# Set-up in order of need in a one-core transformer block kernel

## The reference

```python
out = jnp.einsum('bnd,ed->bne', patches, W) + b + pos
q, k, v = src @ Wq.T + bq, src @ Wk.T + bk, src @ Wv.T + bv
scores = jnp.einsum('bid,bjd->bij', q, k) / sqrt(64)
out = softmax(scores) @ v @ Wo.T + bo      # rows masked where q or k is 0 in column 0
h = layernorm(h + attention(h))
h = layernorm(h + ffn(h))    # top-1 of 8 experts, relu, capacity, weight by the gate
```

## Time and profile before

| | |
|---|---|
| median of 3 runs | 1059.79 us (1058.4 to 1060.67) |
| profiled execution | 1059.04 us, of which span 1057.1 us |
| instructions | 19754 |
| PE / DVE / ACT / POOL busy | 90% / 82% / 67% / 60% of the span |
| first set-up step of DVE | 9.67 us |
| first query-key product on PE | 14.25 us |
| first row maximum on DVE | 27.79 us |
| first product of scores on PE | 42.38 us |

### The profile page before, as it was taken

How to read it: one execution, slowest core, us unless ns; L and a number is a source line. 1 busy time by engine, 2 the same in 40 slices (tenths; PEclk the granted TensorE clock), 3 DMA queues, 4 the chain that set the end, 5 groups by cost and what they waited for, 6 DMA issues and landing times.

```text
span 1057.1 us, 19754 instructions
## 1 busy us (share of the span) xinstructions
PE 947.4 (90%) x6046; PEld 530.7 (50%) x6046; DVE 871.8 (82%) x1711; ACT 712.3 (67%) x1254; POOL 635.8 (60%) x624
## 2 busy tenths in 40 slices
PE   3799999999999999999999999999999999856740
PEld 2355545555555555555555555555555555433420
DVE  3667788789999999999999999999999999675561
ACT  2366655777777777777777777777777776636650
POOL 0004443346666666667776766666666777776775
PEclk9699999999999999999999999999999999958875
DMA  3332224333334333343334333433334332236200
GB/s 95 80 73 58 59 59 107 91 100 101 98 86 120 89 107 99 89 106 103 103 99 107 102 99 86 120 88 107 98 91 106 102 99 72 71 92 177 71 20 10
DMA packets 72504, 96.25 MB, mean 91 GB/s; under 512 B 15923, under 2 KB 52230, under 8 KB 72398
## 3 DMA queue, kind: packets, MB, share of 16 engines
q1 hardware_dynamic: 55566, 77.87, 29.0%
q0 software_dynamic: 16832, 17.11, 5.0%
HBM read 43.68 MB, written 18.11 MB: 58 GB/s over the span
## 4 chain that ended last, share of the span: by engine, by line
PE 48%; DVE 34%; issue 9%; ACT 7%; DMA 1%; POOL 1%; SPq 0%; POOLq 0%; ACTq 0%; DVEq 0%
PE p_u L603 12%; DVE mx L1031 9%; PE p_st L581 8%; PE p_misc L618 6%; PE p_misc L549 4%; PE p_misc L666 3%; PE p_sm L563 3%; PE p_misc L526 3%; ACT uu L809 3%; PE p_st L585 3%; DVE qk L1016 2%; DVE lo L1023 2%; ACT b_h L855 2%; PE p_sm L682 2%; PE p_misc L682 2%
## 5 line engine op out<-in xcount | busy, mean ns | idle before, releaser
L1411 POOL DMA_INDIRECT slots<-rows,idx x256 | 251.9, 984 | 186.2 <-issue 139.6
L1424 POOL DMA_INDIRECT out<-b_o,b_ix x270 | 303.8, 1125 | 98.0 <-issue 74.1
L1031 DVE TENSOR_REDUCE mx<-p_sm 128x1 f32<-128x1024 f32 x252 | 307.1, 1219 | 33.2 <-PE p_sm L565 30.1
L804 ACT ACTIVATE pT<-p_st 128x1024 f32<-128x1024 f32 x256 | 261.9, 1023 | 94.0 <-PE p_st L587 80.1
L603 PE MATMUL p_u<-pT,vv 128*64 128x512 f32 x1024 | 253.5, 605 | 0.0
L581 PE MATMUL p_st<-hi,hx 64*128 64x512 f32 x256 | 126.6, 495 | 8.6 <-ACT pT L804 4.4
L583 PE MATMUL p_st<-hx,hi 64*128 64x512 f32 x256 | 127.1, 496 | 0.0
L603 PEld LDWEIGHTS p_u<-pT,vv 128*64 128x64 f32 x1024 | 61.6, 136 | 104.7 <-issue 92.7
L581 PEld LDWEIGHTS p_st<-hi,hx 64*128 64x128 f32 x256 | 46.9, 183 | 131.3 <-issue 104.0
L563 PE MATMUL p_sm<-kh,hi 64*128 64x512 f32 x252 | 102.4, 406 | 6.1 <-DMA hx<-hi 3.5
L855 ACT ACTIVATE b_h<-p_misc,b_w 128x256 f32<-128x256 f32 x244 | 95.8, 475 | 13.5 <-PE p_misc L666 7.1
(11 more groups left out here) (191 smaller groups left out, 1869.7 us busy)
## 6 DMA issues: line engine op xcount, KB each, us to landing
b_w<-in_w SPq DMA_DIRECT2D x136, 193.5 KB
hx<-hi SPq DMA_DIRECT2D x64, 256.0 KB, 3.4
b_in<-slots SPq DMA_DIRECT2D x136, 66.0 KB
lx<-lo SPq DMA_DIRECT2D x32, 256.0 KB, 3.2
xt<-in_x SPq DMA_DIRECT2D x32, 196.0 KB
out<-b_o,b_ix POOLq DMA_INDIRECT x270, 2.3
kh<-kh SPq DMA_DIRECT2D x32, 128.0 KB, 2.3
lx<-lo SPq DMA_DIRECT2D x32, 128.0 KB, 3.2
```

Of the source, the lines that this page charges most:

```text
L804: act.activation(pT[k % 4][:, :], flat(p_st), ACT.Exp).then_inc(exp_done, 1)
L1031: dve.tensor_reduce(mx[:, p, at:at + 1], flat(max_place(n, j)), AX.X, ALU.max).then_inc(max_done, 1)
L1411: pool.indirect_dma_start(slots, bass.IndirectOffsetOnAxis(ap=idx[:, p, j:j + 1], axis=0), rows[:, p, j, :], None, bounds_check=SLOTS - 1, ...
L1424: pool.indirect_dma_start(out_rows, bass.IndirectOffsetOnAxis(ap=b_ix[:, o, j:j + 1], axis=0), b_o[:, o, j, :], None, bounds_check=T - 1, ...
```

## The change

Loads are issued in another order and with signals of their own: `c_deep` and `w_qk` (`deep_loaded`), the position table for tile 0 alone (`pos_loaded`), the patches of image 0, then `c_wide` and the positions of tiles 1 and 2 (`w_loaded`, now two transfers). The set-up makes `w_qkx` in its first round; the products behind `w_cg`, `w_lj`, `w_all` and `w_px` move behind the first query-key product. The constants that come from `c_wide` are made last. `key_steps(0)` moves in between. The first of image 0's two `hx` transfers has a semaphore of its own. `project(0, .., 1)` is cut into two halves at k = 2 and 3. Identity blocks of `w_lj` come from `c_deep`.

```diff
--- before.py
+++ after.py
@@ -264,10 +264,13 @@
             return back_place(c).rearrange("p (j u d) -> p u j d", j=CT, d=D)
 
 
+        deep_loaded = sem("deep_loaded")
+        pos_loaded = sem("pos_loaded")
         w_loaded = sem("w_loaded")
         x_loaded = [sem(f"x_loaded{i}") for i in range(3)]
         spread_kh = [sem(f"spread_kh{i}") for i in range(2)]
         spread_hi = [sem(f"spread_hi{i}") for i in range(3)]
+        spread_first = sem("spread_first")
         spread_lo = [sem(f"spread_lo{i}") for i in range(3)]
         free_stored = sem("free_stored")
         table_step = sem("table_step")
@@ -337,7 +340,7 @@
         last_rows_ready = sem("last_rows_ready")
         POOL_SET = 2
         GS = 13
-        NW = 4
+        NW = 2
 
         def of_parity(n, p, per):
 
@@ -388,10 +391,12 @@
         @block.sync
         def _(sp):
 
+            sp.dma_start(c_deep[:, :], deep).then_inc(deep_loaded, 16)
+            sp.dma_start(w_qk[:, :], wqk).then_inc(deep_loaded, 16)
+            sp.dma_start(xt[0:D, 0, :], posT).then_inc(pos_loaded, 16)
             sp.dma_start(xt[KA:KTOK, 0, :], x[0, :, :]).then_inc(x_loaded[0], 16)
-            for dst, src in ((c_deep[:, :], deep), (w_qk[:, :], wqk),
-                             (xt[0:D, :, :], posT.unsqueeze(1).broadcast_to([D, 3, S])), (c_wide[:, :], wide)):
-                sp.dma_start(dst, src).then_inc(w_loaded, 16)
+            sp.dma_start(c_wide[:, :], wide).then_inc(w_loaded, 16)
+            sp.dma_start(xt[0:D, 1:3, :], posT.unsqueeze(1).broadcast_to([D, 2, S])).then_inc(w_loaded, 16)
             for n in (1, 2):
                 sp.dma_start(xt[KA:KTOK, n, :], x[n, :, :]).then_inc(x_loaded[n], 16)
 
@@ -455,8 +460,9 @@
                 sp.wait_ge(hi_ready, n + 1)
                 if n >= 3:
                     sp.wait_ge(st_done, NT * (n - 2))
-                for dst, src in ((hx[t][D:P, :], hi[t][0:D, :]), (hx[t][0:D, :], hi[t][D:P, :])):
-                    sp.dma_start(dst.bitcast(F32), src.bitcast(F32)).then_inc(spread_hi[t], 16)
+                sp.dma_start(hx[t][D:P, :].bitcast(F32), hi[t][0:D, :].bitcast(F32))\
+                    .then_inc(spread_first if n == 0 else spread_hi[t], 16)
+                sp.dma_start(hx[t][0:D, :].bitcast(F32), hi[t][D:P, :].bitcast(F32)).then_inc(spread_hi[t], 16)
 
             def spread_low(n):
                 t = n % 3
@@ -495,27 +501,36 @@
         @block.tensor
         def _(pe):
 
-            pe.wait_ge(w_loaded, 16 * NW)
+            pe.wait_ge(deep_loaded, 32)
             pe.wait_ge(setup_v, 1)
-            pe.matmul(p_misc[0:D, 0, 0:D], w_v[:, :], w_oTp[:, :], start=True, stop=True)
-            pe.matmul(p_misc[0:D, 1, 0:E], c_centre[:, :], w_g[:, :], start=True, stop=True)
-            pe.matmul(p_sm[0:D, 0, 0:1], w_oTp[:, :], w_bv[:, :], start=True, stop=True)\
+            pe.matmul(p_u[0:KTOK, 0, 0:2 * D], w_e[:, :], w_qk[:, :], start=True, stop=True)\
                 .then_inc(setup_p, 1)
             pe.wait_ge(setup_v, 2)
-            pe.matmul(p_st[0:KA, 0, 0:CG], w_bl[:, :], w_cg[:, :], start=True, stop=True)
-            pe.matmul(p_st[:, 1, 0:CG], w_lj[:, :], w_cg[:, :], start=True, stop=True)\
+            pe.matmul(p_sm[0:D, 0, 0:D], w_v[:, :], w_oTp[:, :], start=True, stop=True)
+            pe.matmul(p_sm[0:D, 1, 0:E], c_centre[:, :], w_g[:, :], start=True, stop=True)
+            pe.matmul(p_st[0:D, 0, 0:1], w_oTp[:, :], w_bv[:, :], start=True, stop=True)\
                 .then_inc(setup_p, 1)
-            pe.matmul(p_u[0:KTOK, 0, 0:2 * D], w_e[:, :], w_qk[:, :], start=True, stop=True)
-            pe.wait_ge(setup_v, 3)
-            pe.matmul(p_u[0:KTOK, 1, 0:GP], w_e[:, :], w_all[:, :], start=True, stop=True)\
-                .then_inc(setup_p, 1)
-            pe.wait_ge(setup_v, 4)
+
+            def projections():
+                pe.wait_ge(setup_v, 4)
+                pe.matmul(p_st[0:KA, 0, 0:CG], w_bl[:, :], w_cg[:, :], start=True, stop=True)
+                pe.matmul(p_st[:, 1, 0:CG], w_lj[:, :], w_cg[:, :], start=True, stop=True)\
+                    .then_inc(setup_p, 1)
+                pe.wait_ge(setup_v, 5)
+                pe.matmul(p_u[0:KTOK, 1, 0:GP], w_e[:, :], w_all[:, :], start=True, stop=True)\
+                    .then_inc(setup_p, 1)
+                pe.wait_ge(setup_v, 6)
 
             def after_qk(n):
 
                 pe.wait_ge(kh_ready, n + 1)
 
             def qk_product(n, p):
+                if n == 0:
+                    pe.wait_ge(pos_loaded, 16)
+                    pe.wait_ge(setup_v, 3)
+                if n == 1:
+                    pe.wait_ge(w_loaded, 16 * NW)
                 pe.wait_ge(x_loaded[n % 3], 16 * (n // 3) + 16)
                 if isinstance(n, int) and n == 1:
                     after_qk(0)
@@ -527,7 +542,7 @@
                                      start=True, stop=True)
                 last.then_inc(qk_done, 1)
 
-            def project(n, p, r, qk_next):
+            def project(n, p, r, qk_next, part=range(4)):
 
                 if r == 0:
                     pe.wait_ge(x_loaded[n % 3], 16 * (n // 3) + 16)
@@ -544,17 +559,21 @@
                     pe.wait_ge(v_ready, 2 * n + 1)
                     if chunk_of(n - 1) is not None:
                         pe.wait_ge(b_relu, 2 * PAIRS * HB * (chunk_of(n - 1) + 1))
-                for j in range(4):
+                for j in part:
                     t = 4 * r + j
                     last = pe.matmul(projected(n, r)[:, j // 2, (j % 2) * GP:(j % 2 + 1) * GP],
                                      xt[0:KTOK, n % 3, t * P:(t + 1) * P], w_px[:, :], start=True, stop=True)
-                last.then_inc(v_done, 1)
+                if 3 in part:
+                    last.then_inc(v_done, 1)
 
             def max_scores(n, j):
                 t = n % 3
                 if j == 0:
                     pe.wait_ge(spread_kh[n % 2], 16 * (n // 2) + 16)
-                    pe.wait_ge(spread_hi[t], 32 * (n // 3) + 32)
+                    if n == 0:
+                        pe.wait_ge(spread_first, 16)
+                    else:
+                        pe.wait_ge(spread_hi[t], 32 * (n // 3) + (16 if t == 0 else 32))
                     after(pe, shift_ready, n)
                     after(pe, pos_read, n - 2)
 
@@ -572,6 +591,8 @@
             def scores(n, k):
                 t = n % 3
                 if k == 0:
+                    if n == 0:
+                        pe.wait_ge(spread_hi[t], 16)
                     pe.wait_ge(spread_lo[t], 32 * (n // 3) + 32)
                     pe.wait_ge(shift_ready, n + 1)
                 after(pe, exp_done, NT * n + k)
@@ -708,6 +729,7 @@
                 if has(-2) and b < NB:
                     positions(b - 2)
                 if b == -1:
+                    projections()
                     project(0, q, 0, True)
                 if has(2):
                     qk_product(b + 2, par)
@@ -729,8 +751,10 @@
                     if back is not None and b <= NB and k == 2:
                         pe.wait_ge(t_ready, min(b, NB))
                         turn_back(back)
-                    if has(1) and (k == 6 or k == 3 and b >= 0):
+                    if has(1) and b >= 0 and k in (3, 6):
                         project(b + 1, q, k // 6, has(2))
+                    if b == -1 and k in (2, 3):
+                        project(0, q, 1, True, range(2 * k - 4, 2 * k - 2))
                     if m is not None and k in (4, 5):
                         up(m, k - 4)
                     if k == 4 and b == NB - 1 or k == 5 and b == NB:
@@ -765,8 +789,6 @@
             act.preload_act_table_set("natural_log_exp_and_others")
             act.wait_ge(const_set, 1)
             act.activation(b_sd[D:KA, 0:1], w_e[D:KA, D:KA], ACT.Copy)
-            act.wait_ge(w_loaded, 16 * NW)
-            act.wait_ge(setup_v, 4)
 
             def qk_copy(n):
                 act.wait_ge(qk_done, n + 1)
@@ -967,37 +989,44 @@
                 ins.then_inc(set_link, 1)
                 dve.wait_ge(set_link, links[0])
 
-            dve.memset(xt[D:KA, :, :], 1.0)
+            def key_steps(n):
+                dve.wait_ge(qk_ready, n + 1)
+                dve.tensor_tensor(qk[D:P, 0:S - P], qk[D:P, 0:S - P], flat(p_misc)[D:P, P:S], ALU.subtract)\
+                    .then_inc(dk_ready, 1)
+
             dve.memset(w_all[:, :], 0.0)
             dve.memset(w_e[D:KA, :], 0.0).then_inc(set_link, 1)
             dve.wait_ge(set_link, 1)
             dve.memset(w_e[D:KA, D:KA], 1.0).then_inc(const_set, 1)
+            dve.memset(xt[D:KA, 0, :], 1.0)
             dve.wait_ge(const_set, 1)
-            dve.wait_ge(w_loaded, 16 * NW)
+            dve.wait_ge(deep_loaded, 32)
+            dve.tensor_copy(w_e[0:D, :], w_t[:, :]).then_inc(setup_v, 1)
             dve.tensor_scalar(w_oTp[:, :], w_oT[:, :], w_oT[:, D - 1:D], None, ALU.subtract)\
                 .then_inc(setup_v, 1)
-            dve.tensor_copy(w_e[0:D, :], w_t[:, :])
```

(33 more changed lines are left out.)

## The result

The changed kernel takes 1052.39 us (median of 6 runs, 1049.02 to 1053.63), the kernel before in the same comparison 1058.88 us (6 runs, 1057.93 to 1060.67). The ratio is 0.9934 with a 95% interval of 0.9922 to 0.9946, faster by 0.5 to 0.8%. The forecast was 1049.0 us in a range of 1045.9 to 1053.2: direction and range hold, and the time lies where rival B stood (1051.9). The profiled execution took 1053.03 us with a span of 1051.1, 6.01 us less than the profiled execution before, where the sum had 10.75.

A forecast was written before the change was run, and what follows sets the result against it. The prediction took a serial run-up before about 42 us, ahead of busy PE loops, as the place to gain: 8.95 + 0.8 + 1.0 = 10.75 us off, giving 1049.0 us against the median of 1059.79, range 1045.9 to 1053.2.

The forecast's parts named there:

- rival B: Run-up: the product of image 1 runs at 1.2 GHz, costing 1.85 us, cut projection's gain likely void; 1051.9 us, chance 0.15.
- Part 1: First wait: set-up waits only for c_deep and w_qk, landing at 3.4 us; gain 6.3 us (4.7 to 6.3).
- Part 2: Order of set-up products: first query-key product at 5.3 instead of 14.25; 8.95 us together with the first wait.
- The second working, by rate: Landing of the patches: first four transfers, 580 KB at 174 GB/s, take 3.3 us, to 4.9.
- rival A: Input loads progress side by side, positions and patches land late; 1053.3 us, or halfway product at 7.4 and 1051.1; chance 0.15.
- Part 3: Work pushed behind the first product: image 1's product at Q + 8.55, taking 1.96; 0.8 us together with the own signal.
- Q: Start of the first query-key product, that of image 0, taken as 5.3 us.
- Part 4: Own hx signal: first maximum could start at Q + 12.35, but key_steps(1) holds it until Q + 12.75.
- Part 5: Projection cut in two among image 0's maxima: first rounds still at 2.4 GHz, gain 1.0 us of 0 to 1.5.
- rival C: The clock holds through the maxima and the product of image 2: 1.7 + 0.5 us more, 1046.8 us; chance 0.12.
- Passing on: Loops behind the run-up wait only on each other, so they pass its gain on one to one.
- Rivals D and E: D: low clock outlasts the run-up, 1064 us, chance 0.03. E: a later wait gives the gain back, 1059.5, chance 0.02.

The follow-up runs named there:

- changed a third time: The changed kernel run again unedited, its third profile; 1052.40 us, 0.9932 of the kernel before.
- 16 zeros: The changed kernel plus 16 products on a tile of zeros (6, 6, 2 and 2) keeping PE busy in the run-up; 1049.89 us, 0.9901 of before.
- 16 and 5: The kernel with 16 zeros plus one product on zeros behind each of rounds 3 to 7 of image 0's maxima; 1048.88 us, 0.9902 of before.
- 16 with one hx signal: The kernel with 16 zeros, with both hx transfers of image 0 on one semaphore again; 1052.19 us, 0.9932 of before.

## Why the prediction was right, and where its sum was off

The direction was right because the run-up was the right place and the loops pass its lead on. The sum had 10.75 us and the profile shows 6.01 (6.5 by the medians); two of its terms failed, the landing of the patches and the product of image 1. By its own parts:

| part | forecast | measured |
|---|---|---|
| 1 and 2, to the first product | 8.95 | 7.28 |
| 3 and 4, to the first maximum | 0.8 | -0.80 |
| 5, maxima and product of image 2 | 1.0 | 0.41 |
| passed on to the end | 0 | -0.88 |

**Part 1** was right: 3.44 for 3.4. **Part 2** had the right releaser among its two candidates and the wrong time: w_qkx is ready at 5.0 as worked out, the patches land 4.3 us after their issue and not in 2.2 to 3.8. They are there at 6.8, where the prediction had 6.2 at the latest, so even the bound of the sum (7.65) was broken. The step that failed is this bound on the landing: 3.8 us was the landing of an hx transfer. A full queue alone isn't the difference, for hx had company too (DMA share 1.00 from 24.0 to 26.9); but as 48 rows and 1 the patches land 3.94 us after their issue, close to it, and as 49 rows 4.3 to 4.9 in the profiles. The prediction had weighed the 49 rows and found no cost beyond its 1.2 us for them; they cost 0.4 to 0.9 us. The second working, by rate, had the volume right (580 KB by 4.9, measured by 5.3) and the order wrong: it took the transfers strictly one after another, and some 370 KB of later ones were moved ahead of the patches' end. That is rival A, given 0.15, about halfway: its 7.4 for the start of the product, measured 6.97 to 7.43.

**Part 3** was right in every start: w_px at Q + 6.16, projection at Q + 6.5 (forecast 6.5), the product of image 1 at Q + 8.5 (8.55), w_loaded landing at 10.45 (10.3) and releasing nothing. It failed in one term, the 1.96 us of that product: rival B, given 0.15. The row at 21.50 showed the product at the high clock behind a dense stretch of PE, and the forecast carried it to a stretch with stops. The zeros show this: with PE kept busy, the same product on the same data takes 1.88 in all three profiles with 16 of them, against 3.32 to 3.62 in the three without.

**Part 4** has the right mechanism and the wrong level of the clock: 0 us measured with the product of image 1 slow, 1.25 us with it fast. The prediction said that the first maximum would be bound by key_steps, not by the transfer, and that is so in the changed kernel.

**Part 5**: the first rounds did start at the high clock, the halves themselves ran at the low one (1.27 and 1.28 us), so 0.41 for 1.0. That the clock would be low again for the product of image 2 held in every profile (3.39 to 3.62 us), so rival C did not occur once.

**Passing on**: right up to the last image (7.6 us of lead), off by 1.4 us in the rounds behind it. The cause is the grant there. From the `b_p` at 973.73 (before) and 966.36 (changed) on, four rounds between one `b_p` and the next can be compared in each of six profiles (before, changed, changed a third time, 16 zeros, 16 and 5, 16 with one hx signal): three of the 24 take 9.6 us, at a grant of 1.00, six take 11.3 at 0.70, and fifteen 10.5 to 11.3 at 0.84 or 0.85. From the fast to the slow ones DVE and ACT stay busy for as long (6.5 to 7.0 and 7.2 us), while PE goes from 5.4 us to between 8.1 and 8.3. Which round is the fast one differs; here is the third one of the kernel with 16 zeros:

```profile
985.75:995.34 9.59, 5.38 (x43) 3.27 (x40) 6.53 (x13) 7.16 (x18) 6.21 (x6) 1.00 0.05 19
```

Nothing shows that the change took the fast round away; it looks like a difference between executions. So single profiles pass the lead on to within 1.4 us: from 6.9 at the first scores to 6.0 at the end, 7.7 to 7.4, 10.6 to 9.2, 9.8 to 10.5 and 7.9 to 7.9 in the five, against the one profile before. Rivals D and E did not occur.

**Luck.** That 1052.39 lies in the range, and within 0.5 us of B's sum (1051.9), is in part luck. B and A halfway came together, and the prediction's own terms for both give 1059.79 - 8.95 + 1.05 + 2.1 = 1054.0, outside the range. What brought it back: A cost 1.7 and not 2.1, part 5 gained 0.4 where B had it void, and the kernel before measured 1058.88 and not 1059.79.

## What to carry to other kernels

In a serial run-up, ask for each gain whether the step that binds next will still wait: in this change the new loads bring the lead; the reordered products bring nothing beside them (and 2.1 us together with the other parts without them), the cut 0.1 to 0.4, and the own signal 1.2 only once the clock was high. What a part is worth when it is taken away last (4.4 us for the loads) is not its share of the whole. A product's duration taken from one place need not hold in another with other work of TensorE in front of it (1.96 and 3.62 us here); filling the stops of this run-up with products on zeros brought 2.5 us more. And a landing time taken from another transfer is no bound for one with another shape and other transfers behind it: 3.1 to 3.8 us there, 4.3 to 4.9 here, with some 370 KB of later transfers moved ahead of its end.
